# A transformer block on one core: its cross half and its own projections in two streams, and heads of a pair on the two halves of the array

## The reference

```
for i in range(NL):                          # NL = 6
    xn = _adaln(x, noise_emb, n1_w[i], n1_b[i])
    q, k, v = split(xn @ qkv_w[i].T); q = _rope(q); k = _rope(k)
    x = x + _attn(q, k, v, src_mask) @ so_w[i].T
    xn = _adaln(x, noise_emb, n2_w[i], n2_b[i])
    q = _rope(xn @ cq_w[i].T); k = _rope(context @ ck_w[i].T); v = context @ cv_w[i].T
    x = x + _attn(q, k, v, ctx_mask) @ co_w[i].T
    xn = _adaln(x, noise_emb, n3_w[i], n3_b[i])
    x = x + (gelu(xn @ f1_w[i].T + f1_b[i]) @ f2_w[i].T + f2_b[i])
```

## Time and profile before

| | |
|---|---|
| median of the runs | 4610.91 us |
| the profiled execution | 4613.32 us |
| its span | 4611.5 us |
| TensorE busy | 4031.0 us (87%) |
| VectorE busy | 3249.7 us (70%) |
| ScalarE busy | 2277.7 us (49%) |
| granted TensorE clock, mean | 0.91 |
| block 1, from first own maximum to last addition | 2135.57 to 3604.28 us |

### The profile page before, as it was taken

How to read it: one execution, slowest core, us unless ns; L and a number is a source line. 1 busy time by engine, 2 the same in 40 slices (tenths; PEclk the granted TensorE clock), 3 DMA queues, 4 the chain that set the end, 5 groups by cost and what they waited for, 6 DMA issues and landing times. The chain is left out here.

```text
span 4611.5 us, 83547 instructions
## 1 busy us (share of the span) xinstructions
PE 4031.0 (87%) x24597; PEld 2622.9 (57%) x24597; DVE 3249.7 (70%) x16939; ACT 2277.7 (49%) x7483; POOL 407.0 (9%) x338
## 2 busy tenths in 40 slices
PE   8999999999999999876888888888887346979897
PEld 6888888888888888653333333333333223644456
DVE  7888888888888888665666666666664455456543
ACT  5555555555555555432655555555555222236432
POOL 0000000000000000011111111111111010024310
PEclk9999999999999999886988888888888667989998
DMA  0000000000000000012122222222220002500001
GB/s 30 2 2 2 2 2 2 2 2 2 2 2 2 2 2 2 15 43 69 27 50 54 50 54 50 54 50 54 49 51 17 5 4 72 139 30 6 11 10 42
DMA packets 92091, 121.98 MB, mean 26 GB/s; under 512 B 28292, under 2 KB 75583, under 8 KB 91396
## 3 DMA queue, kind: packets, MB, share of 16 engines
q1 hardware_dynamic: 91651, 116.82, 10.0%
HBM read 85.42 MB, written 30.53 MB: 25 GB/s over the span
## 5 line engine op out<-in xcount | busy, mean ns | idle before, releaser
L297 DVE CUSTOM_DVE_ANT_0 I-197junk<-I-193encw,I-196expo,I-205rec 128x77 f32<-128x77 f32 x3072 | 945.6, 356 | 7.0
L1335 DVE TENSOR_REDUCE I-41263nmax<-ps 128x1 f32<-128x512 f32 x768 | 500.9, 686 | 201.8 <-PE ps L1003 192.0
L1223 ACT ACTIVATE I-41266prob<-ps 128x512 f32<-128x512 f32 x768 | 428.4, 595 | 238.1 <-PE ps L1040 235.5
L275 ACT ACTIVATE I-195tanh_s<-ps 128x77 f32<-128x77 f32 x1024 | 241.3, 236 | 594.9 <-PE ps L255 594.9
L255 PEld LDWEIGHTS ps<-I-190hist,I-49small 128*128 128x128 f32 x2048 | 304.6, 188 | 298.3 <-DVE I-190hist L333 298.3
L255 PE MATMUL ps<-I-190hist,I-49small 128*128 128x77 f32 x2048 | 456.4, 304 | 0.2
L261 PE MATMUL ps<-I-195tanh_s,I-49small 128*128 128x77 f32 x2048 | 454.6, 304 | 0.0
L262 PE MATMUL ps<-I-190hist,I-49small 128*128 128x128 f32 x2048 | 439.5, 296 | 0.0
L257 PE MATMUL ps<-I-190hist,I-194uh_h 128*128 128x128 f32 x2048 | 439.5, 296 | 0.0
L283 ACT ACTIVATE I-201hh<-I-207gate_t,I-206pre,I-200rh 128x1 f32<-128x1 f32 x1024 | 395.5, 386 | 88.0 <-DVE I-206pre L297 0.2
L1003 PE MATMUL ps<-I-41257kS,I-41256qS 96*128 96x512 bf16 x768 | 346.2, 470 | 83.0 <-DVE I-41263nmax L1335 58.0
(11 more groups left out here) (542 smaller groups left out, 7062.9 us busy)
## 6 DMA issues: line engine op xcount, KB each, us to landing
I-41256qS<-parts SPq DMA_DIRECT2D x96, 192.0 KB, 4.9
parts<-I-41275room SPq DMA_DIRECT2D x36, 384.0 KB, 2.5
parts<-I-41275room SPq DMA_DIRECT2D x36, 256.0 KB, 2.1
I-41257kS<-parts SPq DMA_DIRECT2D x48, 192.0 KB, 4.6
I-61029spread<-gates_rows SPq DMA_DIRECT2D x24, 256.0 KB, 4.1
I-61030spread<-gates_rows SPq DMA_DIRECT2D x22, 256.0 KB, 4.1
I-61031spread<-gates_rows SPq DMA_DIRECT2D x22, 256.0 KB, 4.0
parts<-I-41275room SPq DMA_DIRECT2D x36, 128.0 KB, 1.8
```

The source lines that it names most:

```text
L297: return e.tensor_tensor_reduce(junk[:, 2 * g + b, :], encw[:, g, b, :], expo[:, b, :], inv[:, b:b + 1], rec[:, b, g:g + 1], ALU.mult, ALU ...
L1223: e.activation(prob[:, tau % 2, j, :], k.ps[:, b, :], ACT.Exp, scale=scale).then_inc(free[b], 1)
L1335: e.tensor_reduce(nmax[:, U % HG, i, j:j + 1], k.ps[:, use[0], :], AX.X, ALU.max, negate=True).then_inc(free[use[0]], 1)
```

## The change

It does four things.

1. Halves. `qS`, `kS` and `cS` become [128, batch, 8, tokens]: head h lies in slot h // 2, at rows 0 to 50 where h is even and rows 64 to 114 where it is odd (`head`). The two maxima rows move to rows 49 and 50 of the half, so the matmuls contract 49 and 51 rows instead of 96 and 128. Neighbouring heads j and j + 1 of a group use different halves and, as before, different banks. In the cross maxima step the four matmuls that write one bank now all have heads of one half (two query tiles, two heads), and the step after it has the other half.
2. The preparing stage fills `kS` and `cS` once, with ones; the fills are half as large; the mask goes out in eight DMAs instead of four.
3. Each spread is cut in two DMAs, one per half: eight instead of four for queries and keys, two instead of one for the context.
4. Streams. `rest` is cut into "x" (cross half and inner layers, banks 5 and 6) and "r" (own projections, bank 7), each with its own semaphores, and "r" with its own buffers (`work`). The rotation gives up its turn between its two products. Context keys come ahead of "ln2". All `TURNS` are new, written out over the whole length with no repeated layer.

```diff
-ROWS_QK = 96
-ROW_MAX = 96
-ROWS_ALL = 128
+ROWS_QK = 49
+ROW_MAX = 49
+ROWS_ALL = 51
@@
-        qS = sbuf(ctx, nc, "qS", [ROWS_ALL, B, NH, T], BF16)
-        kS = sbuf(ctx, nc, "kS", [ROWS_ALL, B, NH, T], BF16)
-        cS = sbuf(ctx, nc, "cS", [ROWS_ALL, B, NH, S], BF16)
+        qS = sbuf(ctx, nc, "qS", [P, B, NH // 2, T], BF16)
+        kS = sbuf(ctx, nc, "kS", [P, B, NH // 2, T], BF16)
+        cS = sbuf(ctx, nc, "cS", [P, B, NH // 2, S], BF16)
+        work = sbuf(ctx, nc, "work", [P, 7 * T])
@@
-                e.memset(kS[:].rearrange("p c h t -> p (c h t)").bitcast(F32), 0.0).then_inc(s.filled, 1)
-                e.memset(cS[:], 0.0).then_inc(s.filled, 1)
-                e.wait_ge(s.filled, 2)
                 for dst in (kS, cS):
-                    e.memset(dst[ROW_MAX:ROW_MAX + 2], 1.0).then_inc(s.filled, 1)
+                    e.memset(dst[:], 1.0).then_inc(s.filled, 1)
@@
-        R = ring(rest_order(), (5, 6, 7))
+        R = dict(chain(ring(cross_order(), (5, 6)).items(), ring(own_order(), (7,)).items()))
@@
+            def head(tile, c, h, rows):
+                return tile[64 * (h % 2):64 * (h % 2) + rows, c, h // 2, :]
@@
-                            e.matmul(k.ps[:, b, :], qS[0:ROWS_QK, c, 4 * m + j, i * P:(i + 1) * P],
-                                     kS[0:ROWS_QK, c, 4 * m + j, :], start=True, stop=True,
+                            e.matmul(k.ps[:, b, :], head(qS, c, 4 * m + j, ROWS_QK)[:, i * P:(i + 1) * P],
+                                     head(kS, c, 4 * m + j, ROWS_QK), start=True, stop=True,
                                      skip_group_check=True).then_inc(full[b], 1)
@@
-                                for j in range(4):
-                                    mm = e.matmul(k.ps[:, b, j * S:(j + 1) * S],
-                                                  qS[0:ROWS_QK, c, 4 * g + j, i * P:(i + 1) * P],
-                                                  cS[0:ROWS_QK, c, 4 * g + j, :], start=(j == 0), stop=True,
-                                                  skip_group_check=True)
+                                for n in range(4):
+                                    y, q = divmod(n, 2)
+                                    x, h = 2 * (i // 2) + y, 4 * g + 2 * q + i % 2
+                                    mm = e.matmul(k.ps[:, b, n * S:(n + 1) * S], head(qS, c, h, ROWS_QK)[:, x * P:(x + 1) * P],
+                                                  head(cS, c, h, ROWS_QK), start=(n == 0), stop=True, skip_group_check=True)
@@
                         for g, landed in enumerate(jsent[name]):
-                            e.dma_start(dst[0:ROW_MASK, c, n * g:n * g + n, :], src[:, n * g:n * g + n, :]).then_inc(landed, 16)
+                            for u in range(2):
+                                e.dma_start(dst[64 * u:64 * u + ROW_MASK, c, n * g:n * g + n, :],
+                                            src[:, 2 * n * g + u:2 * n * g + 2 * n:2, :]).then_inc(landed, 16)
@@
-                weave(TURNS["tensor"], m=all_of(maxima), a=all_of(attend), r=all_rest(rest))
+                weave(TURNS["tensor"], m=all_of(maxima), a=all_of(attend), x=all_cross(rest), r=all_own(rest))
```

More of the change, by code:

```diff
@@ L726 @@
[L726 to L736, removed]
@@ L1304, in rest @@
                             yield
-                    if r < NA:
+                    if part == "r":
                         centre("ln1")
@@ L1376, in attend, with rest @@
                     yield
-                def rest(r):
+                def rest(part, r):
+                    stats, aggr, var, rstd, shifted, centred = lanes[part]
                     c, l = r % B, (r - B) // B
@@ L1583, in rest @@
                         yield
-                    if c == 0 and r >= B and nl < NL:
+                    if part == "r" and c == 0 and r >= B:
                         e.wait_ge(s.wk_in, 16 * nl)
@@ L1589, in rest @@
                         yield
-                    if c == 1 and nl < NL:
+                    if part == "r" and c == 1:
                         e.wait_ge(s.wq_in, 32 * (nl + 1))
@@ L1683, in rest @@
                             yield
-                    if r < NA:
-                        yield from deliver("k", 0, T, kS, K_SPOTS)
-                        yield from deliver("q", 1, T, qS, Q_SPOTS)
-                weave(TURNS["sync"], m=all_of(maxima), r=all_rest(rest))
+                    if part == "r":
+                        yield from deliver("k", 2, T, kS, K_SPOTS)
+                        yield from deliver("q", 3, T, qS, Q_SPOTS)
+                weave(TURNS["sync"], m=all_of(maxima), x=all_cross(rest), r=all_own(rest))
 def add_stream(nc, x, z):
```

348 lines of the change are left out of this document (195 added, 153 removed), and 2 rows, old and new, of the table SPOT.

## The result

| | before | after |
|---|---|---|
| median of 4 runs | 4611.67 us (4610.57 to 4613.62) | 4823.06 us (4812.42 to 4826.64) |
| span of the profiled execution | 4611.5 us | 4823.0 us |
| one cycle (of nine) | 121.6 us | 139.8 us |
| low clock (1.2 GHz) in a cycle | 32.2 us | 71.3 us |
| mean granted clock over the nine cycles | 0.87 | 0.74 |

The ratio is 1.0454 (95% interval 1.0436 to 1.0472). I had forecast 4532, with 0.12 on slower. The time is far above my range.

What follows compares the result with a forecast made beforehand. A cycle was taken as bound by VectorE, then TensorE, then a dependent chain. Nine cycles x 6 us, two end cycles at 3 each and 18.3 preparing gave 78 us off: 4532 us, range 4460 to 4628.

Steps and rivals of the forecast that it cites:

- The preparing stage: Before the cycles: shorter fills let TensorE's first matmul come 18.3 us earlier, bounds 12 to 21.
- the second rival: Score and maxima matmuls of opposite halves don't run at once: 0 gained a cycle, 4592 us; chance 0.21.
- The chain behind "ln3": Dependent steps up to the next cycle's first maximum: three and a half fewer scores there save 2.4 us a cycle.
- The clock stays low: Slower rival: TensorE runs at 1.2 GHz for 24 us more a cycle, total 4647 us; chance 0.13.
- B: Cycle stretch of 65.5 us with maxima, scores, cross-attention and inner layers; TensorE, busy 62.5 us, bounds it.
- the three faster cases: The forecast (0.46), no holes left (4475 us, 0.20) and the halves not running at once (4592 us, 0.21).
- The 7.4 us for the pairs: In the TensorE-bound stretch, 37 pairs of opposite-half matmuls a cycle overlap, saving 0.20 us each.
- the change of shape: Trips between halved and full-array matmuls: 19 a cycle at up to 0.24 us, 2.3 us lost, bounds 0 and 4.6.
- 7.4 + 1 - 2.3: Per cycle in us: pairs in the TensorE-bound stretch, plus pairs in the dependent chain, less changes of shape.
- this shift: Maxima beside the inner layers move ahead of "ln3", leaving fewer scores behind it: 2.4 us saved, bounds 0 and 6.
- a floor of 2.4 us: Ahead of "ln3" VectorE needs 66 us against TensorE's 63.6, so it takes back 2.4 us a cycle.
- A and B: The cycle's first two stretches: 16.5 us of maxima only, bound by VectorE, then 65.5 us bound by TensorE.

Runs made afterwards that it cites:

- rows49: The kernel before, one head per slot, with matmuls contracting 49 and 51 rows instead of 96 and 128: 4929.03 us, ratio 1.0685.
- halves: The kernel before with the change's halved layout, fills and split spreads (49 and 51 rows), but order, streams and banks of before: 4698.27 us, ratio 1.0171.
- halves64: halves with 62 and 64 rows of each half contracted instead of 49 and 51, the added rows zero: 4646.86 us, ratio 1.0078 against the kernel before.
- rows65: The kernel before, one head per slot, with matmuls contracting 65 and 67 rows instead of 96 and 128: 4715.49 us, ratio 1.0202.
- old_full: halves, but contracting whole slots (112 and 128 rows, both heads at once), leaving out head separation, for time only: 4591.34 us, ratio 0.9949 against the kernel before.
- early: The kernel before with 14 of the fourth group's 16 maxima matmuls moved ahead of "ln3" in six cycles: 4667.48 us, ratio 1.0117.
- order_full: The changed kernel, but contracting whole slots (112 and 128 rows, both heads at once), leaving out head separation: 4693.25 us, ratio 1.0170 against the kernel before.
- fills126: The kernel before with one-pass fills (keys ones, queries zeros then ones) and maxima over 126 rows, order unchanged: 4589.00 us, ratio 0.9945.

## Why the prediction was wrong

**Right.** The preparing stage (18.3 forecast, 17.9 measured). Pairs of opposite halves start together, so the second rival, that the halves don't run at once, is out. The cut spreads cost nothing that could be told. The chain behind "ln3" got shorter by the order, from 56.3 to 54.9 us with whole rows; I had 2.4 us.

**Failed first: the weight of "The clock stays low".** The mechanism was named, its sign (more than 30 us a cycle at 0.50) was named, and it came with more than the 24 us I priced: 39 more a cycle after, 30 more by the layout alone. I argued against it with TensorE's idle time: "B was at 62.5 of 65.5". The runs show that this is the wrong thing to look at. rows49 is 98% busy in that stretch at 0.57, and in one order, with the same DMAs and trips, the low clock goes from 62 to 44 us a cycle when each matmul uses 62 and 64 rows instead of 49 and 51 (halves, halves64). Nothing in the trace of before could have shown that, since its maxima always use 96 rows and its scores 128. But it was an unshown behaviour on which the whole gain of the halves hung, and 0.13 for it, below the three faster cases together at 0.87, was too sure.

The price per us was near what I wrote, and smaller: against before, a us more of low clock comes with 25.5 / 58.1 = 0.44 us of cycle in rows49 (changes of shape included), 4.4 / 11.8 = 0.37 in rows65, 9.7 / 29.6 = 0.33 in halves. A part of the low clock lies where VectorE is the bound: the first stretch of before, 21.03 us, has VectorE busy 18.54 at a clock of 0.57.

**The 7.4 us for the pairs** did not come as a shorter cycle, and the change of shape was sized too small: 0.29 us a trip (rows49 against rows65), where I had 0.20 to 0.24 and took half of it. What the pairs bring at the full clock no run shows by itself: no kernel had the halves without more low clock. But halves64 can be laid beside rows65, with nearly the same rows (62 and 64, 65 and 67), the same order, the same 44.0 us of low clock a cycle, and neither pairs nor trips. Nine cycles of rows65, then of halves64:

```profile
2368.55:3502.82 1134.27, 977.31 (x4954) 390.23 (x4952) 714.00 (x1485) 612.93 (x1170) 153.95 (x149) 0.83 0.20 48
```

```profile
2325.72:3460.42 1134.70, 948.49 (x4954) 359.69 (x4952) 714.38 (x1486) 611.36 (x1170) 151.64 (x149) 0.83 0.15 48
```

TensorE is busy 3.2 us less in a cycle, and the cycle is as long: 126.0 and 126.1 us. Where TensorE is the bound, from the first score to "ln3", halves64 takes 45.0 us for 47.7 in the mean of nine cycles; in the chain behind it takes 59.7 for 56.8. So pairs and trips together brought nothing, where the sum had 7.4 + 1 - 2.3. The cut spreads don't lengthen the chain (56.3 us in old_full). How much of the 2.9 us are trips, and how much the low clock in the chain (12.1 us for 8.3), stays open.

**Failed second: "Nothing is removed by the streams alone; what an own buffer and an own bank allow is this shift".** I credited the end of the shift, fewer scores in the chain, and took its other end as free but for a floor of 2.4 us. In the order before, the maxima beside the inner layers cost nothing, since there neither VectorE nor TensorE is the bound. Moved ahead of "ln3" they cost their own time: in early, 15 instructions of VectorE, 8.8 us busy, 9.0 us of the stretch. I added the busy times of VectorE in A and B and compared the sum with TensorE's path, as if either could be filled to the end; in early that stretch is 52.84 us with VectorE busy 41.82. With whole rows the new order's stretches ahead of "ln3" grew by 9.8 us a cycle and the chain gave 1.4 back.

**Missed in the order: ScalarE's tables.** Over nine cycles ScalarE loads its tables for Gelu 14 times instead of 9, and 14 instead of 9 for the exponential behind it, because exponentials now stand between hidden tiles. Before (groups by line, nine cycles), then after:

```profile
L1302 ACT ACT_TABLE_LOAD x9 | 11.5, 1283 | 0.2
```

```profile
L1343 ACT ACT_TABLE_LOAD x14 | 18.0, 1283 | 0.2
```

That is 10 x 1.283 = 12.8 us of ScalarE, 1.4 us of its time in a cycle. I could have counted it from the new string. It was not tried alone. What the rest of the order's waiting ahead of "ln3" is made of, some 5 us a cycle with whole rows, stays open, and so does how much of the 9.5 us of low clock a cycle that order_full has above old_full is cause and how much is consequence.

**The sum, redone.** Layout in the old order +83 us (107 lost on the halved matmuls, 24 won, of which the preparing stage is 18), order and streams +102, and a remainder of +27 that only both together give: 212 us, against the measured 211.4. The remainder is the difference, not a measured term.

## What to carry to other kernels

Dividing the array between two matmuls pays only if the clock survives it: try the fewer rows alone first, in the old order, as rows49 does with three constants and the fills that belong to them, and see whether the granted clock holds. Unused rows of zeros can be worth keeping. Work in the shadow of a chain of dependent steps was free here and cost its whole duration ahead of the chain; when an order is rewritten, price both ends of every move, and count the table loads that it makes.

## What was not expected of the hardware

- The granted clock depends on how many rows a matmul contracts: 90, 44 and 32 us of low clock a cycle for 49, 65 and 96 rows of maxima, with the same matmuls in the same order (29 with 126 is hardly to be told from 32). Rows of zeros count: halves64 adds nothing but zeros and takes 18 us of low clock off a cycle.
- TensorE can be busy 62.19 of 63.17 us and be granted 0.57.
- A trip from halved matmuls over a projection of all rows and back costs 0.29 us at the full clock: 1.37 us with 49 rows for 1.08 with 65.
- 16 more matmuls of 96 rows in a stretch of low clock did not raise its clock (0.57 both times, busy 14.42 and 19.74 us); they cost 2.2 us a cycle.
- The mask's 1178 elements on VectorE took 0.76 us before, 1.62 after and 3.87 us in fills126. GpSimd had ended its fills before the first, and filled beside the other two; that this is the cause was not tried alone. The fill in fills126:

```profile
2058.21 6.92 POOL L875 MEMSET I-41256qS<- 49x8192 f32 x1
```
